# Attention output and scores that change the column half at every matmul, and low rank gate products spread over array parts

## The reference

```python
H, DK, DV, LOW_RANK, GATE_NORM, CHUNK = 4, 128, 64, 16, 16.0, 64
q = (x @ Wq).reshape(B, T, H, DK)
k = (x @ Wk).reshape(B, T, H, DK)
v = (x @ Wv).reshape(B, T, H, DV)
gk = jax.nn.log_sigmoid(x @ Wgk1 @ Wgk2 + bgk2) / GATE_NORM      # Wgk1: 256x16, Wgk2: 16x512
G = jnp.cumsum(gc, axis=-2)                                      # in chunks of 64 tokens
qg = qc * jnp.exp(G) * scale
k_intra = kc * jnp.exp(-G)
A = jnp.einsum('nbhik,nbhjk->nbhij', qg, k_intra)                # scores, 64x64 per chunk and head
A = jnp.where(jnp.tril(jnp.ones((C, C), bool)), A, 0.0)
o_intra = jnp.einsum('nbhij,nbhjv->nbhiv', A, vc)
o = oi_ + jnp.einsum('bhck,bhkv->bhcv', qg_, S)                  # in the scan over chunks
S = S * gl_[..., :, None] + jnp.einsum('bhck,bhcv->bhkv', kg_, v_)
o = o * rsqrt(mean(o * o) + EPS) * gnw * (g * sigmoid(g))
return o.reshape(B, T, H * DV) @ Wo
```

## Time and profile before

| | |
|---|---|
| median of 3 runs | 1844.66 us (1843.87 to 1845.01) |
| the profiled execution | 1847.26 us, with a span of 1845.5 us |
| PE busy | 1696.9 us, 92% of the span |
| DVE, ACT, POOL busy | 80%, 74%, 74% |
| blocks 3 to 15 | one every 80.5 us |
| granted PE clock, 200 to 1280 us | 1.00 of full speed |

### The profile page before, as it was taken

The page is one execution under the profiler, slowest core; times in us unless marked ns, Lnnn a source line. Parts: engine busy times, 40 slices in busy tenths (PEclk is TensorE's granted clock), DMA queues, the critical chain, the costliest instruction groups (busy, mean ns, idle before and its releaser), DMA issues.

```text
span 1845.5 us, 33565 instructions
## 1 busy us (share of the span) xinstructions
PE 1696.9 (92%) x12092; PEld 1454.0 (79%) x12092; DVE 1475.3 (80%) x3084; ACT 1362.8 (74%) x2673; POOL 1369.7 (74%) x644
## 2 busy tenths in 40 slices
PE   6788999999999999999999999998776999999998
PEld 5566787888878888787888878787565888899997
DVE  3557898898989889888988988888898678766663
ACT  3458879888887988888788888877643756666664
POOL 0008899998989989898998989899999333444443
PEclk8989999999999999999999999999998999999999
DMA  4011121122122112212211221212213444555552
GB/s 195 1 34 65 59 75 66 58 75 82 48 86 75 70 53 75 82 56 82 72 70 61 67 82 61 82 61 80 69 52 99 130 105 108 137 138 137 135 135 29
DMA packets 69461, 149.76 MB, mean 81 GB/s; under 512 B 5936, under 2 KB 43312, under 8 KB 68912
## 3 DMA queue, kind: packets, MB, share of 16 engines
q1 hardware_dynamic: 57008, 130.84, 20.6%
q0 software_dynamic: 12288, 16.79, 5.2%
HBM read 121.91 MB, written 17.30 MB: 75 GB/s over the span
## 4 chain that ended last, share of the span: by engine, by line
PE 73%; DVE 7%; issue 7%; POOL 6%; ACT 6%; DMA 0%; POOLq 0%; DVEq 0%; ACTq 0%
PE po L1820 10%; PE ph L1820 9%; PE pD L1118 9%; PE pY L1135 8%; PE pA L722 6%; DVE room L1167 3%; POOL room L1176 3%; PE pB L914 3%; PE pB L924 3%; POOL room L1186 3%; PE pB L1214 3%; PE pB L945 2%; PE pA L621 2%; PE pA L656 2%; PE pB L930 2%
## 5 line engine op out<-in xcount | busy, mean ns | idle before, releaser
L1186 POOL TENSOR_TENSOR room<-room 128x1024 f32<-128x1024 f32 x256 | 607.2, 2372 | 168.7 <-DVE room L1101 144.0
L1167 DVE TENSOR_TENSOR_SCAN room<-pD,last,room 128x256 f32<-128x256 f32 x1024 | 690.1, 732 | 43.0 <-PE pD L1118 31.7
L1176 POOL TENSOR_TENSOR room<-room 128x1024 f32<-128x1024 f32 x256 | 607.3, 2373 | 62.1 <-PE pY L1135 61.5
L1148 ACT ACTIVATE room<-room,fixed,kkT 128x512 f32<-128x512 f32 x512 | 406.6, 807 | 54.7 <-PE pD L1118 52.7
L1118 PE MATMUL pD<-fixed,room 128*128 128x128 f32 x2048 | 316.6, 278 | 60.3 <-DVE room L1167 49.1
L1135 PE MATMUL pY<-fixed,room 128*128 128x128 f32 x2048 | 315.5, 277 | 11.4 <-POOL room L1176 11.4
L1118 PEld LDWEIGHTS pD<-fixed,room 128*128 128x128 f32 x2048 | 240.0, 143 | 93.2 <-issue 44.1
L1135 PEld LDWEIGHTS pY<-fixed,room 128*128 128x128 f32 x2048 | 246.6, 144 | 61.6 <-POOL room L1176 24.1
L341 POOL DMA_INDIRECT xg<-xn_rows,W x64 | 67.5, 1054 | 196.5 <-DVE W L335 181.0
L1779 ACT ACTIVATE h<-ph 128x512 f32<-128x512 f32 x128 | 76.7, 599 | 137.8 <-PE ph L1820 107.1
L1820 PE MATMUL po<-w_up,h_up 128*128 128x256 f32 x512 | 149.6, 292 | 3.2 <-DVE h_rest L1687 2.6
(11 more groups left out here) (313 smaller groups left out, 3507.4 us busy)
## 6 DMA issues: line engine op xcount, KB each, us to landing
room<-kq_rows SPq DMA_DIRECT2D x128, 512.0 KB, 3.9
w_in<-w_d SPq DMA_DIRECT2D x32, 1024.0 KB
room<-ndS SPq DMA_DIRECT2D x16, 512.0 KB, 3.2
xt<-x_in SPq DMA_DIRECT2D x16, 256.0 KB, 2.9
y_out<-xo SPq DMA_DIRECT2D x16, 256.0 KB, 2.1
xn_rows<-xnC SPq DMA_DIRECT2D x16, 256.0 KB, 2.2
W<-weights SPq DMA_DIRECT2D x1, 1808.0 KB, 9.5
W<-weights SPq DMA_DIRECT2D x1, 1697.5 KB, 17.1
```

What stands on the lines that cost most here:

```text
L1148: act.activation(decT[:, m % 2, t, :], turn2(ndT, it, NT * DI, t * DI, DI), ACT.Identity, bias=ones_s[:, 0:1], scale=turn2(kkT, it, NT * D ...
L1167: dve.tensor_tensor_scan(run, pD[h][:, k2 * TB:(k2 + 1) * TB], run, last[:, bass.ds(later(it) * (DS * DT) + m * DT + k, 1)], ALU.mult, ALU ...
L1176: pool.tensor_tensor(sq[:, m % 2], st[:, m % 4], kqb[:, m % SLOTS, 1, :].unsqueeze(1).broadcast_to([P, DT, TB]), ALU.mult).then_inc(sem("r ...
L1186: pool.tensor_tensor(st[:, m % 4], turn2(u, it, DT * TB).rearrange("p (k t) -> p k t", k=DT), kqb[:, m % SLOTS, 0, :].unsqueeze(1).broadca ...
```

## The change

The order of the matmuls of `o` is turned round: pairs of heads outside, chunks next, and inside a chunk first the two matmuls with S of the pair's two heads, then the two with the scores. So each matmul goes to the other column half than the one before it. The scores go through token tiles, heads, chunks of the tile, with the same effect. The low rank product is split by token tile: tile t goes to output partitions 32t to 32t+15, so that one matmul of 256 columns becomes two of 128 on different column parts. `lr` becomes a tile of 64 rows and 128 columns, the second weight is laid out twice (rows 0 to 16 and 32 to 48), and z's two matmuls read different row parts of the array. ACT copies `lr` in two instructions. Semaphores and steps stay as they are.

```diff
@@ scores_of
-                for c in range(NCH):
-                    for h2 in range(2):
-                        h, at = 2 * hp + h2, (c // 2 * 2 + h2) * CH
-                        i = pe.matmul(pA[hp][c % 2 * CH:(c % 2 + 1) * CH, at:at + CH],
-                                      kin[:, h, c * CH:(c + 1) * CH], qg[:, h, c * CH:(c + 1) * CH],
-                                      start=True, stop=True)
+                for t, h2, c2 in itertools.product(range(NT), range(2), range(2)):
+                    c, h, at = 2 * t + c2, 2 * hp + h2, (t * 2 + h2) * CH
+                    i = pe.matmul(pA[hp][c2 * CH:(c2 + 1) * CH, at:at + CH],
+                                  kin[:, h, c * CH:(c + 1) * CH], qg[:, h, c * CH:(c + 1) * CH],
+                                  start=True, stop=True)
@@ low
-                    i = pe.matmul(pA[1][0:LR, 0:TB], wgk1[:, c, :], hA[:, c, :], start=(c == 0), stop=(c == DC - 1))
+                    for t in range(NT):
+                        i = pe.matmul(pA[1][t * LRQ:t * LRQ + LR, 0:P], wgk1[:, c, :], hA[:, c, t * P:(t + 1) * P],
+                                      start=(c == 0), stop=(c == DC - 1), skip_group_check=True)
@@ z
-                    pe.matmul(pA[t][:, :], lr[0:LR + 1, t * P:(t + 1) * P], wgk2[0:LR + 1, :], start=True, stop=True)\
+                    rows = slice(t * LRQ, t * LRQ + LR + 1)
+                    pe.matmul(pA[t][:, :], lr[rows, :], wgk2[rows, :], start=True, stop=True)\
@@ o
-                for h in range(H):
-                    hp, h2 = h // 2, h % 2
+                for hp in range(2):
                     for c in range(NCH):
-                        o = pA[0][h2 * DV:(h2 + 1) * DV, hp * TB + c * CH:hp * TB + (c + 1) * CH]
-                        pe.matmul(o, S[:, 1 + c, h * DV:(h + 1) * DV], qg[:, h, c * CH:(c + 1) * CH], start=True, stop=False,
-                                  skip_group_check=True)
-                        i = pe.matmul(o, vh[:, c // 2, c % 2, h * DV:(h + 1) * DV], att[:, c // 2, h, :],
-                                      start=False, stop=True, skip_group_check=True)
+                        for h2 in range(2):
+                            h = 2 * hp + h2
+                            pe.matmul(o_of(hp, c, h2), S[:, 1 + c, h * DV:(h + 1) * DV], qg[:, h, c * CH:(c + 1) * CH],
+                                      start=True, stop=False, skip_group_check=True)
+                        for h2 in range(2):
+                            h = 2 * hp + h2
+                            i = pe.matmul(o_of(hp, c, h2), vh[:, c // 2, c % 2, h * DV:(h + 1) * DV], att[:, c // 2, h, :],
+                                          start=False, stop=True, skip_group_check=True)
@@ ACT, lr
-                act.activation(lr[0:LR, :], pA[1][0:LR, 0:TB], ACT.Copy).then_inc(sem("lr"), 1)
+                for t in range(NT):
+                    rows = slice(t * LRQ, t * LRQ + LR)
+                    i = act.activation(lr[rows, :], pA[1][rows, 0:P], ACT.Copy)
+                i.then_inc(sem("lr"), 1)
```

More of the change, by code:

```diff
@@ L2 @@
 from contextlib import ExitStack
+import itertools
 import numpy as np
@@ L49 @@
 XBUF = 4
+LRQ = 32
 KV_SCALE = 2.0 ** -12
@@ L442, in layers @@
         hA = sb("hA", [P, DC, TB])
-        lr = sb("lr", [2 * LR, TB])
+        lr = sb("lr", [NT * LRQ, P])
         lz = w_in[:, 0:NT * H * DK]
@@ L692, in attn_pe, with o_of @@
                 pe.wait_ge(sem("state"), it * 16 + 16)
-                for h in range(H):
-                    hp, h2 = h // 2, h % 2
+                def o_of(hp, c, h2):
+                    return pA[0][h2 * DV:(h2 + 1) * DV, hp * TB + c * CH:hp * TB + (c + 1) * CH]
+                for hp in range(2):
                     for c in range(NCH):
-                        o = pA[0][h2 * DV:(h2 + 1) * DV, hp * TB + c * CH:hp * TB + (c + 1) * CH]
-                        pe.matmul(o, S[:, 1 + c, h * DV:(h + 1) * DV], qg[:, h, c * CH:(c + 1) * CH], start=True, stop=False,
-                                  skip_group_check=True)
-                        i = pe.matmul(o, vh[:, c // 2, c % 2, h * DV:(h + 1) * DV], att[:, c // 2, h, :],
-                                      start=False, stop=True, skip_group_check=True)
+                        for h2 in range(2):
[6 more added lines that the diff above has]
+                                          start=False, stop=True, skip_group_check=True)
                 i.then_inc(sem("o_mm"), 1)
@@ L1919, in spaced, with per_tile @@
         return np.concatenate([x[:, :DR], gap, x[:, DR:]], axis=1)
+    def per_tile(x):
+        gap = np.zeros((LRQ - x.shape[0], x.shape[1]), np.float32)
+        return np.concatenate([x, gap] * NT, axis=0)
     def pair(x):
@@ L1927 @@
         "wv": rows_of_chunks(a["L0_attn_Wv"]), "wg": rows_of_chunks(a["L0_attn_Wg"]),
-        "wgk1": rows_of_chunks(a["L0_attn_Wgk1"]), "wgk2": rows_of_chunks(np.concatenate([a["L0_attn_Wgk2"], a["L0_attn_bgk2"][None]])),
+        "wgk1": rows_of_chunks(a["L0_attn_Wgk1"]), "wgk2": rows_of_chunks(per_tile(np.concatenate([a["L0_attn_Wgk2"], a["L0_attn_bgk2"][None]]))),
         "win2": rows_of_chunks(two(a["L0_ffn_Win"])), "inproj": rows_of_chunks(a["L1_attn_in_proj_w"].T),
```

## The result

The changed kernel takes 1827.05 us, the median of 6 runs (1822.35 to 1830.43); the kernel before, in runs beside them, 1844.36 (1842.62 to 1845.01). The ratio is 0.9907, with a 95% interval of 0.9895 to 0.9918: 17.3 us, or 0.9%, faster. The forecast of the median was 1827.4 us. The profiled execution took 1829.17 us, with a span of 1827.4 us against 1845.5; that the span shows the figure of the forecast is chance.

What follows compares the result with a forecast made beforehand. PE, 92% busy, and POOL were taken as nearly full. Steady blocks 11.7, opening 5.3 and last `o` 0.3 make 17.3 us: 1847.3 - 17.3 = 1830.0, less 2.6 (profiled over median) 1827.4 us; range 1812 to 1838.

Steps and rivals of the forecast that it cites:

- the 11.7 counted: Steady part: thirteen blocks, each about 0.9 us shorter, 11.7 us in all.
- a gain of 0.3: Behind the steady part: 0.3 us saved by the last block's `o`.
- (a): Rival, chance 0.16: column parts overlap, row parts don't; low alone passes, 0.14 at the first sum; 10.5 us, so 1834.
- (c): Rival, chance 0.05: only row parts overlap, so only z gains, 0.58 us a block; 1836 us.
- (e): Rival, chance 0.03: slower; each change of column part drains the array, 0.09 us; 3.0 us a block, 1893 us.
- (b): Rival, chance 0.12: the saving reaches the end nearly whole; 1.9 to 2.64 us a block, 1814 or 1805 us.
- (d): Rival, chance 0.12: ACT or DVE hold the period at every point; only the opening gains, 4 to 5.3 us; 1840.
- `o` is tied at ACT: Attention's end: ACT reaches the square without idle time, so of 1.3 us saved in `o` only 0.29 shortens the path.
- low and z pass up to POOL: Sum behind z waits for POOL's product: of 1.29 us saved 0.58 passes, 0.7 becomes a wait there.
- PE can come forward by 0.14 up to the first: At PE's sum at 633.74, which waits for POOL's product ending at 633.60: 0.14 us of slack.
- The opening: Blocks 1 to 3, where PE isn't full: savings in `o`, `low` and z, together 5.3 us.
- the 0.87 of my sum: Steady block: 0.29 + 0.58 + 0.05 - 0.05 = 0.87 us saved, from `o`, low and z, scores, less DVE's hold.

Runs made afterwards that it cites:

- an edit that did nothing before: Two step table numbers altered (ACT's inverse root two steps earlier, DVE's layer norm sums two later): kernel before 1843.73 us, changed kernel 1821.89 us.

## Why the prediction was right, and where it wasn't

The time, 1827.4, was met to 0.4 us. The mechanism held in its main points; the near hit of the number is partly luck. The steady part gave 13.2 us for the 11.7 counted, what lies behind it lost 0.4 for a gain of 0.3, the profiled executions lie 18.1 us apart by their spans and the medians 17.3, and the change's own runs spread over 8 us.

- **Column and row parts work together.** `o` 2.02 us (predicted 2.05), `low` -0.40 (-0.43), z -0.85 (-0.86), scores -0.05 each (both together were taken as 0.05). For z no row of before had shown it, and the value by the nearest rows was right. Of the rivals (a), (c) and (e) nothing is left, and (b) and (d) fall with the period: it gained 1.04 us, where (b) had 1.9 or more and (d) nothing. The rule of the Trainium skill (TensorE: Matmul & The Clock Gate, Part 3) that a weight load passes a running matmul "only when row_grp differs" is not what these runs show, neither for the column halves nor for the loads: in `o` all matmuls use all rows, and 64 passes start within 1.86 us where they took 3.19; and already before a weight load's record is 0.14 us long while passes start every 0.058.
- **`o` is tied at ACT.** Shown by the new order alone (0.40 for 1.3) and by the change of half at every fourth matmul (0.6 us more of `o`, no longer period). The term was 0.29 and measured 0.40. I had read 0.29 as the wait in front of the decay, but a wait's bracket starts only at the end of the record before it; between the two starts 0.97 us had passed where 0.57 are enough. The difference of starts would have given the right size, and any later kernel has it to compare with.
- **low and z pass up to POOL.** 0.53 measured, 0.58 less 0.05 predicted, and z alone gives it all. That the 0.05 fits is luck: it was meant for DVE, and it is what lies between the end of POOL's product (704.71 + 2.36 = 707.07) and the start of the sum (707.13). But the step "PE can come forward by 0.14 up to the first" sum failed: low alone moves the period by 0.03, and its gain is lost ahead of that sum, half of it at a `dec` two sums after `low` that waits for DVE's scan, not for POOL. DVE holds back 0.20 there, not 0.05. It did no harm to the total, since z alone frees more than the 0.58. The wait for POOL shows as 0.29 us, not 0.7: `low`'s 0.40 never reached it.
- **The scores** give 0.09 or 0.10 a block together and not 0.05.
- **The copy on ACT** is hidden, as forecast: twice as many cost no period.
- **PE's busy time** fell by 33.8, not by 40. In one block it fell by 2.10, where the starts of the rows give 1.32 + 0.40 + 0.85 + 0.10 = 2.67. A wait shorter than the tail that each record shows behind its last start (0.60 to 0.66 long rows at a distance of 0.44) still counts as busy; that this is where the 0.6 went I only argue.
- **The opening.** Its sum, 5.3 us (the terms add up to 5.2), was met in this profile (the third `o` starts at 200.43 instead of 205.70) and came to 4.5 in the second profile of the changed kernel (201.25). By blocks it is 3.17, 2.15 and nothing, against 0.9, 2.15 and 2.15 as I had it. The rows of the chains of the two openings show why, before and then after:

```profile
43.81 4.52 PE pA L722 x16
...
139.08 1.98 PE pA L713 x8
```

```profile
41.68 3.47 PE pA L731 x16
...
133.00 3.26 PE pA L722 x8
```

The same 16 passes take 1.05 us less in the first block, and the same 8 of Wo 1.28 more in the second, at 0.41 us a pass instead of 0.25. The granted clock goes with it: over the 16 passes it was 0.78 before and 1.00 after, over the 8 of Wo 1.00 before and 0.58 after, the lower of TensorE's two levels for most of them. The forecast had counted the work and not the clock; that its sum fits is chance.

A steady block gained 1.04 for the 0.87 of my sum. The thirteen steady intervals are 13.2 us shorter together (1046.4 before, 1033.2 now; one of them gained 0.77 only). With 5.3 of the opening that is 18.5, and the span is 18.1 shorter: the drain and the experts give back 0.4 us, where I had taken a gain of 0.3. From the last `o` to the end it is 593.4 us before, 593.8 in the changed kernel and 592.4 in its second profile, so 0.4 can't be told from nothing.

## What to carry to other kernels

Matmuls that leave half of the array's columns free, or most of its rows, ran in pairs here when the matmul for the other part came within two matmuls in program order. For `o` and the scores it was enough to reorder them, and grouping by head was what prevented it; the low rank products had to be laid out for it. Before counting such a saving, look who takes the result next: here 2.67 us off the busiest engine were worth 1.04, because ACT, DVE and POOL each came free just then, and the difference of starts around the next engine's instruction gives the size better than the idle time in front of it. Once the matmuls are short, try the neighbours' order again: an edit that did nothing before (0.9996) was then worth another 5 us.

## What the runs showed of the hardware

- How far PE reaches over to the other half: with the half changing at every 8th, 4th, 2nd and at every matmul the 64 passes of `o` start within 3.19, 2.47, 1.91 and 1.86 us. That fits a reach of two matmuls (four passes) and no more.
- Two float32 matmuls of 17 rows and 512 columns, on different row parts and into different banks, start their four passes within 0.54 us instead of 1.39, two steps of some 0.43 less: nearly complete overlap.
- The granted clock of the opening isn't the same in two executions of one kernel (0.96 and 0.93 in the stretch above), and the third block of the changed kernel came 0.8 us apart. A single profile's opening can't tell a change of a us; the steady block tells 0.02.
